# Queries, keys and softmax transposed as two 64-row halves into two banks, in a fused attention and gated MLP kernel

## The reference

```python
def attn_layer(x, Wqkv, qs, ksc, Wo):          # 16 heads of 64, window 32
    q, k, v = split(x @ Wqkv, 3)
    q = rotary(l2norm(q) * qs); k = rotary(l2norm(k) * ksc)
    # each token sees its own window of 32 and the one before it
    sim  = einsum('bhwie,bhwje->bhwij', bq, bk2) * 8.0      # masked
    attn = softmax(sim, -1)                                 # 64 keys per token
    out  = einsum('bhwij,bhwje->bhwie', attn, bv2)
    return out.reshape(b, n, 1024) @ Wo
def ffn_layer(x, g, bln, W1, b1, W2, b2):
    a, gate = split(layernorm(x) * g + bln @ W1 + b1, 2)
    return a * gelu(gate) @ W2 + b2
for i in range(6):
    x = attn_layer(shift_tokens(x), ...) + x
    x = ffn_layer(shift_tokens(x), ...) + x
```

## Time and profile before

| what | value |
|---|---|
| median of 3 runs | 3991.84 us (3988.7 to 3993.46) |
| the profiled execution's own time | 3979.11 us |
| its span, first to last instruction | 3977.3 us |
| mean granted TensorE clock | 0.965 |
| busy: PE, PEld | 3528.5 us (89%), 2531.4 us (64%) |
| busy: DVE, ACT, POOL | 3481.0 us (88%), 2616.5 us (66%), 2522.5 us (63%) |
| the chain that ended last | PE 53%, ACT 21%, issue 20% |

### The profile page before, as it was taken

The page is one execution under the profiler, slowest core; times in us unless marked ns, Lnnn a source line. Parts: engine busy times, 40 slices in busy tenths (PEclk is TensorE's granted clock), DMA queues, the critical chain, the costliest instruction groups (busy, mean ns, idle before and its releaser), DMA issues.

```text
span 3977.3 us, 158623 instructions
## 1 busy us (share of the span) xinstructions
PE 3528.5 (89%) x60708; PEld 2531.4 (64%) x60708; DVE 3481.0 (88%) x7219; ACT 2616.5 (66%) x4783; POOL 2522.5 (63%) x2671
## 2 busy tenths in 40 slices
PE   6887799998998989989989989989989889899997
PEld 3444476666666666666666666666666666666665
DVE  7888898998898988889989988889889889888895
ACT  3445676776676766667767676666667667666675
POOL 3334576766666766666667666666667667666673
PEclk9878899999999999999999999999999999999998
DMA  2000111112211112211111211112211112211112
GB/s 66 5 5 4 25 49 44 48 44 54 66 42 50 42 49 55 59 50 42 50 42 54 67 42 50 42 42 67 53 47 45 47 45 60 61 42 45 47 44 60
DMA packets 126086, 184.83 MB, mean 46 GB/s; under 512 B 26742, under 2 KB 49332, under 8 KB 124724
## 3 DMA queue, kind: packets, MB, share of 16 engines
q1 hardware_dynamic: 125492, 175.28, 17.2%
HBM read 21.32 MB, written 2.10 MB: 6 GB/s over the span
## 4 chain that ended last, share of the span: by engine, by line
PE 53%; ACT 21%; issue 20%; DVE 4%; ACTq 1%; POOL 0%; DMA 0%; DVEq 0%; SPq 0%; POOLq 0%
PE bank L1066 13%; PE bank L1210 10%; PE bank L1089 9%; PE bank L1152 6%; ACT L615 6%; ACT oT L574 4%; ACT gl L623 4%; PE bank L1167 4%; PE bank L972 2%; ACT znT L612 2%; ACT L626 2%; ACT vt L568 2%; PE bank L1144 2%; PE bank L1013 1%; PE bank L1120 1%
## 5 line engine op out<-in xcount | busy, mean ns | idle before, releaser
L436 POOL TENSOR_TENSOR qk<-ta,tb 128x512 f32<-128x512 f32 x768 | 971.6, 1275 | 513.3 <-DVE tb L814 513.3
L552 ACT ACTIVATE sq<-bank 128x512 f32<-128x512 f32 x768 | 459.3, 598 | 777.9 <-PE bank L1066 771.2
L1066 PE MATMUL bank<-wqkv,zsT 128*128 128x512 f32 x1536 | 831.1, 624 | 114.0 <-issue 104.9
L445 POOL TENSOR_TENSOR qk<-qk,rn 128x512 f32<-128x512 f32 x768 | 776.5, 1042 | 72.9 <-DVE rn L841 72.9
L814 DVE TENSOR_TENSOR ta<-bank,rot 128x512 f32<-128x512 f32 x768 | 529.4, 689 | 259.5 <-ACT sq L552 259.3
L478 POOL TENSOR_TENSOR P<-P,rowsum 128x512 f32<-128x512 f32 x384 | 393.6, 1044 | 498.9 <-DVE rowsum L930 498.9
L814 DVE TENSOR_TENSOR tb<-bank,rot 128x512 f32<-128x512 f32 x768 | 523.0, 681 | 0.0
L1089 PEld LDWEIGHTS bank<-cst,qk 128*128 128x128 f32 x3072 | 376.4, 146 | 214.4 <-issue 213.6
L1210 PE MATMUL bank<-wo,oT 128*128 128x128 f32 x3072 | 393.6, 281 | 130.3 <-ACT oT L574 130.2
L1210 PEld LDWEIGHTS bank<-wo,oT 128*128 128x128 f32 x3072 | 357.4, 191 | 167.1 <-ACT oT L574 128.5
L926 DVE TENSOR_REDUCE ss<-sq 128x32 f32<-128x2048 f32 x192 | 437.0, 2276 | 0.0
(11 more groups left out here) (135 smaller groups left out, 6924.6 us busy)
## 6 DMA issues: line engine op xcount, KB each, us to landing
vs<-vt SPq DMA_DIRECT2D x1152, 128.0 KB, 2.4
wqkv<-L_ffn_Wqkv SPq DMA_DIRECT2D x6, 1024.0 KB, 4.9
wqkv<-L_ffn_Wqkv SPq DMA_DIRECT2D x6, 512.0 KB, 3.8
wo<-L_ffn_Wo SPq DMA_DIRECT2D x6, 512.0 KB, 4.2
z_sb<-x SPq DMA_DIRECT2D x4, 512.0 KB, 6.8
ctxb<-ctx SPq DMA_DIRECT2D x32, 64.0 KB, 1.7
out<-x_sb SPq DMA_DIRECT2D x8, 256.0 KB, 3.5
w<-L_ffn_W SPq DMA_DIRECT2D x6, 341.0 KB, 3.0
```

Of the source, the lines that this page charges most:

```text
L436: g.tensor_tensor(o, i0, i1, ALU.add).then_inc(s["g_add"], 1)
L445: g.tensor_tensor(q3, q3, r3, ALU.mult).then_inc(s["g_qk"], 1)
L552: a_.activation(sq[:, 512 * j:512 * j + 512], bank[j % 2][:, :], ACT.Square)\
L1066: t_.matmul(bank[j % 2][:, :], zsT[:, k % 4, :], wqkv[:, 512 * j:512 * j + 512], start=True, stop=True).then_inc(s["p_qk"], 1)
```

## The change

Each group of transposes is rewritten. The 128 tokens are split in two halves of 64 rows. For each of the eight pairs of heads there are now two transposes: tokens 0 to 63 into bank 4 and tokens 64 to 127 into bank 5, each with 64 rows x 128 columns of weights and 64 columns of the identity moving. The loop alternates between the two halves. The results in the two banks are the same data in another arrangement, and ACT's copies (as many, of the same size) write 8 pieces of 64 columns in place of 4 pieces of 128.

With each half of a group spread over all eight pairs, both increments of `p_tr` (or `p_PT`) stand at the group's end, on its last two instructions. The waits become those of the whole group: both parts of the queries must be normalised before the first transpose, both copies of the queries must be out before the first transpose of keys, and both parts of the softmax must be there. A `nop` on PE takes these waits ahead of each group.

```diff
-                    wait(pool, "p_tr", count(4, a - 2, j + 1))
+                    wait(pool, "p_tr", count(4, a - 2, 2 * (j // 2) + 2))
...
-                    i = 4 * (j % 2)
-                    a_.activation(dst[:, i:i + 4, :], bank[4 + j % 2][:, :].rearrange("p (h q) -> p h q", h=4),
+                    o = 64 * (j % 2)
+                    a_.activation(dst[:, :, o:o + 64], bank[4 + j % 2][:, :].rearrange("p (h q) -> p h q", h=PAIRS),
                                   ACT.Copy).then_inc(s["a_tr"], 1)
...
-                        a_.activation(PT[:, 4 * j:4 * j + 4, :], bank[4 + j][:, :].rearrange("p (h q) -> p h q", h=4),
+                        a_.activation(PT[:, :, 64 * j:64 * j + 64],
+                                      bank[4 + j][:, :].rearrange("p (h q) -> p h q", h=PAIRS),
                                       ACT.Copy).then_inc(s["a_PT"], 1)
...
-                def transpose_qk(j):
-
-                    wait(pe, "g_qk", count(4, b, j + 1))
-                    if j < 2:
-                        edge(pe, n, "a_tr", count(4, b - 1, j + 3))
-                        wait(pe, "a_AV", count(2, c - 1, j + 1))
+                def transpose_rows(src, sem_name):
+
+                    for p in range(PAIRS):
+                        for t in range(2):
+                            tok = slice(64 * t, 64 * t + 64)
+                            ins = t_.transpose(bank[4 + t][:, 64 * p:64 * p + 64], src[tok, 128 * p:128 * p + 128],
+                                               ident[tok, tok])
+                            if p == PAIRS - 1:
+                                ins.then_inc(s[sem_name], 1)
+
+                def transpose_qk(i):
+
+                    wait(pe, "g_qk", count(4, b, 2 * i + 2))
+                    if i == 0:
+                        edge(pe, n, "a_tr", count(4, b - 1, 4))
+                        wait(pe, "a_AV", count(2, c - 1, 2))
                     else:
-                        wait(pe, "a_tr", count(4, b, j - 1))
-                    for p in range(4):
-                        ins = t_.transpose(bank[4 + j % 2][:, 128 * p:128 * p + 128],
-                                           qk[:, pb, 512 * j + 128 * p:512 * j + 128 * p + 128], ident)
-                    ins.then_inc(s["p_tr"], 1)
+                        wait(pe, "a_tr", count(4, b, 2))
+                    pe.nop(nofuse=True)
+                    transpose_rows(qk[:, pb, 1024 * i:1024 * i + 1024], "p_tr")
...
                 if c_on:
-                    for j in range(2):
-
-                        wait(pe, "g_P", count(2, c, j + 1))
-                        edge(pe, n, "a_tr", count(4, b, 4))
-                        edge(pe, n, "a_AV", count(2, c - 1, 2))
-                        for p in range(4):
-                            hp = 4 * j + p
-                            ins = t_.transpose(bank[4 + j][:, 128 * p:128 * p + 128],
-                                               P[:, pc, 128 * hp:128 * hp + 128], ident)
-                        ins.then_inc(s["p_PT"], 1)
+
+                    wait(pe, "g_P", count(2, c, 2))
+                    edge(pe, n, "a_tr", count(4, b, 4))
+                    edge(pe, n, "a_AV", count(2, c - 1, 2))
+                    pe.nop(nofuse=True)
+                    transpose_rows(P[:, pc, :], "p_PT")
```

More of the change, by code:

```diff
@@ L1112, in slot @@
                     transpose_qk(0)
-                    transpose_qk(1)
                 if d_on:
@@ L1124, in slot @@
                 if b_on:
-                    transpose_qk(2)
-                    transpose_qk(3)
+                    transpose_qk(1)
                 if a_on:
```

## The result

The change makes the kernel slower. The median of four runs is 4121.73 us (4117.19 to 4126.68), that of four runs of the kernel before on the same chip 3992.65 us (3988.70 to 4025.35). The ratio is 1.0305, 95% interval 1.0249 to 1.0361. The forecast was 3996 us with a range up to 4060, so the result lies outside it. The profiled execution took 4118.83 us with a span of 4117.0; before it was 3979.1 with 3977.3, so the traces have 139.7 us to explain.

What follows compares the result with a forecast made beforehand. PE bounds each 17.16 us slot's first stretch, ACT the second. Delayed copies and PE's gains sum to 0.00 us, plus 0.02 for uncovered costs: +4 us over 192 units, median 3996 us, no change; range 3950 to 4060.

Steps and rivals of the forecast that it cites:

- A pair costs 0.06 us: In each transpose group, two halves side by side are bound by their weight load: 0.06 us, against 0.11 for a full transpose.
- The rival without overlap: In each transpose group, halves do not run side by side: 0.114 us a pair, +1.2 us a slot, 4222 us; chance 10%.
- The change of form costs 0.09 us: On PE around each group: 0.09 us per switch; with uncovered loads, entering 0.15 us, leaving to a float32 product 0.19.
- the third rival: On PE around the groups, switching between half and full rows is nearly free: -115 us, 3880 us; chance 8%.
- The queries' copies 0.12 us later: ACT's first copy of the queries starts at 2191.95 against 2191.83, since it waits for the whole group.
- The key copies 0.07 later: ACT's copies of the keys start at 2194.08 against 2194.01 and end at 2195.16.
- The masks 0.04 earlier: PE starts the scores' masks 0.05 us after the last key copy, at 2195.21 against 2195.25.
- The softmax 0.04 later: Softmax's transposes: seven pairs to the last end, 0.79 us after entry against 0.75 before.
- ACT's second stretch unchanged: The slot's later part, where ACT sets the pace, stays 8.0 us; copying in 64-column pieces costs nothing.
- The own case: Whole kernel: the forecast's own sum holds, steady slot 17.1 to 17.25 us, 3996 us; chance 55%.
- Small costs stay uncovered: In each group, the nop delays loads or increments and copies meet: 0.05 us, +0.15 a slot, 4021 us; chance 12%.
- The clock: PE's half-clock stretches behind loop boundaries change with slot length, not with transposes: up to 35 us won or lost; chance 15%.

Runs made afterwards that it cites:

- b_real44: Kernel before, full transposes, with 44 real PE instructions (22 extra transposes) run once in the prologue: 4055.66 us, ratio 1.0113.
- p_only: Row halves in the softmax's transposes alone, queries and keys as in the kernel before: 4095.42 us, ratio 1.0238 to before.
- b_flat640: Kernel before with the hardware loop written out and two identity transposes more per slot (640 PE instructions): 3766.88 us, ratio 0.9423.
- b_in44: Kernel before with 44 PE nops written at the head of each loop body: 4010.06 us, ratio 1.0034.
- a_real228: Changed kernel with 228 real PE instructions (114 extra transposes) run once in the prologue: 4074.51 us, ratio 1.0154 to the kernel before.
- qk_only: Row halves in the transposes of queries and keys alone, softmax's full as in the kernel before: 3973.33 us, ratio 0.9945 to before.
- b_flat640_s64: Kernel before, loop written out, two identity transposes more per slot, plus 64 real PE instructions in the prologue: 3892.65 us, ratio 0.9748.
- a_shift232: Changed kernel with 232 PE nops written into the prologue: 4116.12 us, ratio 1.0316 to the kernel before.
- a_shift64: Changed kernel with 64 PE nops written into the prologue: 4116.78 us, ratio 1.0327 to the kernel before.
- b_shift44: Kernel before with 44 PE nops written into the prologue: 3992.33 us, ratio 1.0008.

## Why the prediction was wrong

**The step that failed** is this sentence of the sum: "The three `nop`s and the 24 more transposes lie under streaming or the 0.09 us". It priced the added instructions by their execution, and left out that they must be brought to PE, and that they shift each instruction behind them against the joints of the pieces. The rows to ask were there: an "issue" share of a fifth of the chain, the idle time in front of the scores in the waits of before, and q8's packets. I took them for the loop's jumps. In place of nothing, the two places where the shifted joints fall cost 149 us of stops in the trace.

**The size of it.** The trace of after has stops of (1.62 + 1.76) x 44 = 149 us in the two places, against 25 x 1.60 + 3 = 43 in before, so 106 more. By b_real44, where 90 us more of stops cost 49 us in the medians, some 58 us of it count. That rate is for stops alone, since b_real44 has no more half clock than before (27 stretches over the loop in each). The steady slots add 0.10 x 192 = 19. The half clock adds 99 us of stretches, and PE work in them takes twice its time (two products span 2.07 us there and 1.02 at full clock): at most 50 us. Together up to 127 of 129 us. The steady slots are measured, the stops are an estimate by the rate of another kernel, the half clock is a bound. No run holds the joints of the changed kernel outside the dense part, so what the halves cost where no joint stops PE is known from steady slots alone.

**The halves themselves.**
- *A pair costs 0.06 us*: right. The view of weight loads and the timeline of PE in one group:

```profile
2242.72 0.58 PEld L1086 LDWEIGHTS bank<-cst,qk 64*128 64x128 f32 x16 [0.76 <-issue]
2242.72 0.71 PE L1086 MATMUL bank<-cst,qk 64*128 64x64 f32 x16
```

  Sixteen loads end 0.58 us after the first began; with a load of 0.14 us at the end that is 7 steps of 0.06 between pairs. The rival without overlap (4222 us) asked for 0.114, and fell. The Trainium skill (TensorE: Matmul & The Clock Gate, LDWEIGHTS) puts a load at its columns divided by 1.2, in ns, whatever its rows. That is an estimate of 107 ns for 128 columns; by it a pair could not take less, and these sixteen loads contradict it.
- *The change of form costs 0.09 us*: right, and the third rival fell. The second projection ahead of the queries' group starts at 2257.30 and streams 0.43 us, and the first half starts at 2257.82. Leaving costs as much as was said: the two products behind the keys' halves span 1.13 us, where two behind full matmuls span 1.02.
- *The queries' copies 0.12 us later*: right; 2258.57 against 2258.55 by the sum.
- *The key copies 0.07 later*: 0.12 measured. *The masks 0.04 earlier*: they come 0.06 later. The last copy ends at 2261.81 and the masks start at 2261.90, so the wait costs 0.09 us and not 0.05. These two terms are 0.05 and 0.04 us too small, and make the slot +0.10 where I had said 0.00 and added 0.02.
- *The softmax 0.04 later*: right.
- *ACT's second stretch unchanged*: right, 2272.24 - 2264.25 = 7.99 us, against 8.01.

The own case, with its steady slot of 17.1 to 17.25 us, was thus off by 15 us in the sum: 17.26 us lies just above it, and this alone would have lain inside the range. "Small costs stay uncovered" (+0.15 us a slot) came nearest to the steady slot, and named the wrong costs. In time it is 101 us too low, and the rival without overlap 100 us too high; none of the rivals held the cause.

**The clock.** The rival said that half-clock stretches come with the length of a slot and that this "does not depend on the transposes". What the traces show them to go with is gaps in PE's work. From 560 us to 60 us before the end, all 28 stretches of before, 41 of the 44 of after and all 63 of p_only begin during a jump's idle time or a stop, or less than 4 us after its end, and b_flat640, which has no jump and hardly a stop, has none. So the change brought more of them with its stops. Not every stop has one behind it, and they last differently long: 3.4 us behind the jumps of before and b_real44, up to 6.8 us in p_only and b_in44, up to 10.2 us in after, a_real228 and qk_only. A window of b_real44 behind a jump and the one after it, and one of p_only, whose queries and keys have full transposes too:

```profile
2273.00:2276.40 3.40, 3.40 (x10) 2.26 (x11) 0.43 (x1) 1.04 (x2) 0.00 (x0) 0.52 0.22 39
2276.40:2279.80 3.40, 3.40 (x27) 2.15 (x32) 3.40 (x10) 2.47 (x6) 1.83 (x2) 1.00 0.55 129
...
1900.84:1907.66 6.82, 5.16 (x15) 3.63 (x16) 1.99 (x5) 1.79 (x3) 0.82 (x2) 0.50 0.24 62
```

b_real44 is back at 2.4 GHz after 3.4 us, p_only after 6.8; PE's idle time at this jump of p_only is 3.7 us, where 2.4 is the rule in before. Halves in the queries and keys are thus not needed for a long stretch. Whether they lengthen it in after, where ten of the sixteen stretches behind jumps last 6.8 us and two 10.2, no run shows.

## What to carry to other kernels

An instruction on a full engine costs more than its execution: it has to be delivered, and it shifts all that is behind it. Before splitting one operation into two on PE, count the instructions of a body (weight loads and the sequencer's own too), find where the idle time named "issue" falls inside a group that waits for nothing, and see whether the places lie multiples of 256 instructions apart; a change of 44 instructions in a prologue was worth 49 us here, and 64 of them 126. Where a hardware loop is short, writing it out (4% here) and making the count of instructions per pass a multiple of 128, with the joints outside the dense part (1.7% more), was worth more here than anything done to the transposes.

## What the runs showed of the hardware

- PE stops for 0.3 to 3.3 us at joints 256 instructions apart, where the joint falls in the scores, in the transposes behind them or just behind these (after the 2459th instruction of a_real228, 0.6 us). PE gets through the 256 instructions of a slot's scores, weight loads counted, in about 1.4 us. Moving the joints out of this part removes the stops (b_flat640); moving one in creates them (b_real44, b_flat640_s64).
- Such a stop ends 1.2 to 1.6 us after a packet of the instruction queue has landed, and the 34 joints of b_flat640_s64 that PE reached later than that didn't stop it.
- The jump back of the loop leaves PE idle for 2.4 us (2.8 in p_only), and it may run at 1.2 GHz for 3.4, 6.8 or 10.2 us behind it.
- `nop`s on PE written into the prologue left no instruction in the program (a_shift232, a_shift64, b_shift44).
- Two transposes of 64 rows each, on the two halves of the array, run side by side: 0.06 us a pair (after). Both steps between half and full rows cost the 0.09 us that the earlier trace rows show for 32 rows.
